# DLRM tower on one Trainium2 core: from pair 8 on, the products with four kept pairs have the batch on partitions and ScalarE sums them

## The reference

```python
e = jnp.stack([tbl_0[ids[:, 0]], ..., tbl_39[ids[:, 39]]], axis=1)   # (512, 40, 64)
i_idx, j_idx = np.triu_indices(40, k=1)
viW = jnp.einsum('bpd,pde->bpe', e[:, i_idx, :], W)                  # W (780, 64, 64)
z = jnp.einsum('bpe,bpe->bp', viW, e[:, j_idx, :])                   # (512, 780)
h = jnp.concatenate([z, dense_ctx], axis=1)                          # (512, 796)
h = jnp.maximum(h @ W_top1 + b_top1, 0.0)                            # (512, 512)
h = jnp.maximum(h @ W_top2 + b_top2, 0.0)                            # (512, 256)
y = h @ W_top3
```

## Time and profile before

| What | Value |
|---|---|
| Median of 3 runs | 370.56 us (369.31 to 371.61) |
| The profiled execution's own time | 369.65 us |
| Its span | 367.8 us |
| TensorE busy (matmul) | 347.9 us, 95% of the span |
| VectorE busy | 259.8 us, 71% |
| ScalarE busy | 38.4 us, 10% |
| GpSimd busy | 154.0 us, 42% |
| Mean granted TensorE clock, share of full speed | 0.991 |

### The profile page before, as it was taken

The page is one execution under the profiler, slowest core; times in us unless marked ns, Lnnn a source line. Parts: engine busy times, 40 slices in busy tenths (PEclk is TensorE's granted clock), DMA queues, the critical chain, the costliest instruction groups (busy, mean ns, idle before and its releaser), DMA issues.

```text
span 367.8 us, 4723 instructions
## 1 busy us (share of the span) xinstructions
PE 347.9 (95%) x1848; PEld 117.8 (32%) x1848; DVE 259.8 (71%) x271; ACT 38.4 (10%) x61; POOL 154.0 (42%) x261
## 2 busy tenths in 40 slices
PE   0999399999999999999999999999999999999997
PEld 0333122333333333333333333333233333333342
DVE  3974971787787877676768877887768787877430
ACT  1011201030100201010010300000000001200132
POOL 6888888027776755344434544243323100000000
PEclk9999879999999999999999999999999999999999
DMA  7378121102641422112112220122022000000000
GB/s 188 139 222 337 22 81 25 27 37 81 223 135 26 130 76 76 16 65 73 46 32 73 70 59 26 65 70 68 12 65 68 5 0 2 0 0 3 0 1 0
DMA packets 11449, 24.29 MB, mean 66 GB/s; under 512 B 3858, under 2 KB 3858, under 8 KB 11299
## 3 DMA queue, kind: packets, MB, share of 16 engines
q1 hardware_dynamic: 7330, 19.79, 16.2%
q0 software_dynamic: 4096, 4.20, 5.4%
HBM read 23.98 MB, written 0.00 MB: 65 GB/s over the span
## 4 chain that ended last, share of the span: by engine, by line
PE 94%; DVE 3%; DMA 1%; issue 1%; ACT 0%; SPq 0%
PE y_ps L472 47%; PE z_ps L495 25%; PE t_ps L424 6%; PE t_ps L451 4%; PE y_ps L503 3%; PE t_ps L442 2%; DVE one_hot L380 2%; PE y_ps L533 2%; PE y_ps L424 2%; PE y_ps L478 2%; DMA ids_all<-in_ids_one_hot 1%; PE t_ps L539 0%; ACT x L315 0%; DVE prod L402 0%; ACT prod L357 0%
## 5 line engine op out<-in xcount | busy, mean ns | idle before, releaser
L402 DVE TENSOR_TENSOR prod<-y_ps,x 128x1024 f32<-128x1024 f32 x190 | 220.9, 1217 | 74.4 <-PE y_ps L472 74.0
L472 PE MATMUL y_ps<-x,w_sb 64*128 64x512 f32 x760 | 180.9, 607 | 0.8 <-issue 0.7
L302 POOL DMA_INDIRECT rows<-in_tbl,ids_sb x128 | 122.6, 958 | 131.4 <-PE y_ps L472 99.1
L472 PEld LDWEIGHTS y_ps<-x,w_sb 64*128 64x128 f32 x760 | 66.7, 186 | 104.3 <-issue 53.3
L495 PE MATMUL z_ps<-prod,selector 128*32 128x512 f32 x780 | 94.9, 602 | 0.0
L495 PEld LDWEIGHTS z_ps<-prod,selector 128*32 128x32 f32 x780 | 20.5, 110 | 67.9 <-issue 34.4
L380 DVE TENSOR_SCALAR one_hot<-ids_all,numbers 128x512 f32<-128x512 int32 x64 | 27.5, 504 | 7.4 <-DMA ids_all<-in_ids_one_hot 7.4
L424 PE MATMUL t_ps<-one_hot,table 128*64 128x512 f32 x96 | 22.9, 633 | 8.8 <-DVE one_hot L380 8.8
L297 POOL MEMSET spacer<- 128x128 f32 x127 | 30.7, 242 | 0.1
L315 ACT ACTIVATE x<-t_ps 128x512 f32<-128x512 f32 x18 | 10.8, 599 | 191.3 <-PE t_ps L442 145.1
L451 PE MATMUL t_ps<-z_sb,w_sb 128*128 128x512 f32 x32 | 15.9, 618 | 0.0
(11 more groups left out here) (30 smaller groups left out, 36.8 us busy)
## 6 DMA issues: line engine op xcount, KB each, us to landing
w_sb<-in_w_units SPq DMA_DIRECT2D x25, 512.0 KB, 3.3
ids_all<-in_ids_one_hot SPq DMA_DIRECT2D x8, 256.0 KB, 4.6
table<-in_small_tables SPq DMA_DIRECT2D x8, 256.0 KB, 5.3
rows<-in_tbl,ids_sb POOLq DMA_INDIRECT x128, 2.5
w_sb<-in_w SPq DMA_DIRECT2D x1, 1792.0 KB, 8.0
w_sb<-in_w SPq DMA_DIRECT2D x1, 512.0 KB, 4.4
ids_sb<-in_ids SPq DMA_DIRECT2D x1, 80.0 KB, 2.2
z_sb<-in_dense_t SPq DMA_DIRECT2D x1, 32.0 KB, 9.5
```

Source lines behind the costliest of these rows:

```text
L302: pool.indirect_dma_start(rows[:, n % ROW_SLOTS, bt, h * D:(h + 1) * D], None, tables[f], bass.IndirectOffsetOnAxis(ap=ids_sb[:, bt, f:f + ...
L402: dve.tensor_tensor(prod[:, at:at + 2, :], y_ps[:, s % Y_SLOTS], leaf, ALU.mult).then_inc(prod_ready, 1)
L472: ins = pe.matmul(y_ps[:, slot, h, :], w_sb[own, c % W_SLOTS, at:at + P], x[own, m, :], start=True, stop=True)
```

## The change

Four pairs, `KEPT` = 1, 3, 5 and 7, keep their gathered rows, with the batch on partitions, in a tile of their own (`kept`). For every k from 8 to 19, the four cross units of k with those pairs are replaced by four "rows" units, one for each block of 128 samples. In a rows unit `x[:, k]` of the block is the weight of the matmul and the matrices (8 partners x 64 columns, tile `w_rows_sb`) are what moves through; the result has the batch on partitions and 8 x 64 columns in each of the slot's two banks. VectorE multiplies it by `kept` into one of 4 slots of `row_prod`. ScalarE then runs 16 copies of 128x64 in place, each with `accum_out` into one column of `z_rows`. Two jobs ("z_turn") of four transposes each bring `z_rows` into two banks of `z_sb`. So 147 units are still summed by the selector (37 rounds), and 48 are rows units; the steps stay 195.

With it go: `w_sb` slots 6 to 4, `rows` slots 6 to 4 beside the kept four, `LEAD` 3 to 5, mix one step earlier, partial jobs every 4 steps, twelve loads of 256 KB for `w_rows_sb` on SyncE's queue, each held until the slot's earlier group is used, and the one-hot tiles share their space with `row_prod`, `w_rows_sb` and `z_rows`. `z_sb` has 7 banks as before.

```diff
+KEPT = (1, 3, 5, 7)
+ROWS_FROM = 8
+ROW_PROD_SLOTS = 4
+ROW_W_SLOTS = 2
-W_SLOTS = 6
+W_SLOTS = 4
-ROW_SLOTS = 6
+ROW_SLOTS = 4
+ROW_LAG = 2
-LEAD = 3
+LEAD = 5
-PARTIAL_EVERY = 6
+PARTIAL_EVERY = 4
 def plan_units():
-        cross = [("cross", m, k) for m in range(k)]
+        own = [("cross", m, k) for m in range(k) if k < ROWS_FROM or m not in KEPT]
         if k % 4 == 3:
-            cross.insert(min(k, 6), ("inner", k // 4))
-        units += cross
+            own.insert(min(k, 6), ("inner", k // 4))
+        if k >= ROWS_FROM:
+            every = (len(own) + BT) // BT if k < NP - 1 else 3
+            for bt in range(BT):
+                own.insert(1 + every * bt, ("rows", k, bt))
+        units += own
...
+    jobs_at[FIRST[ROWS_FROM + GROUPS_IN_BANK] + 8].append(("z_turn", 0))
+    jobs_at[STEPS - 2].append(("z_turn", 1))
...
         def _(act):
+            def sum_rows(s):
+                _, k, bt = UNITS[s]
+                act.wait_ge(prod_ready, s + 1)
+                for h in range(2):
+                    for n in range(2 * len(KEPT)):
+                        own = row_prod[:, NUMBER[s] % ROW_PROD_SLOTS, h, D * n:D * n + D]
+                        column = row_sum(k, h, n)
+                        ins = act.activation(own, own, ACT.Copy, accum_out=z_rows[:, bt, column:column + 1])
+                ins.then_inc(rows_summed, 1)
...
+                if s >= ROW_LAG and UNITS[s - ROW_LAG][0] == "rows":
+                    sum_rows(s - ROW_LAG)
...
         def _(dve):
+                if unit[0] == "rows":
+                    if n >= ROW_PROD_SLOTS:
+                        dve.wait_ge(rows_summed, n - ROW_PROD_SLOTS + 1)
...
+                    leaf = kept[:, unit[2]:unit[2] + 1, :, :].rearrange("p o n d -> p o (n d)").to_broadcast([P, 2, B])
+                    dve.wait_ge(y_ready, s + 1)
+                    dve.tensor_tensor(row_prod[:, n % ROW_PROD_SLOTS], y_ps[:, s % Y_SLOTS], leaf,
+                                      ALU.mult).then_inc(prod_ready, 1)
+                    return
...
         def _(pe):
+                if unit[0] == "rows":
+                    _, k, bt = unit
+                    for h, own in enumerate((low, high)):
+                        ins = pe.matmul(y_ps[:, slot, h, :], x[own, k, P * bt:P * bt + P],
+                                        w_rows_sb[own, (k - ROWS_FROM) % ROW_W_SLOTS, :], start=True, stop=True)
+                    ins.then_inc(y_ready, 1)
+                    return
```

More of the change, by code:

```diff
@@ L74 @@
 STEPS = len(UNITS)
[L75 to L81, removed]
+SUMMED = [s for s, u in enumerate(UNITS) if u[0] != "rows"]
+ROWED = [s for s, u in enumerate(UNITS) if u[0] == "rows"]
+NUMBER = {s: n for units in (SUMMED, ROWED) for n, s in enumerate(units)}
+CHUNKS = -(-len(SUMMED) // CHUNK)
+ROUNDS = -(-len(SUMMED) // ROUND)
+EARLY_BANKS = 2 * PARTIAL_PAIRS
+ROW_BANKS = (EARLY_BANKS, EARLY_BANKS + 1)
+BANKS = EARLY_BANKS + 3
+ROW_GROUPS = NP - ROWS_FROM
+GROUPS_IN_BANK = P // ROW_SUMS
+REST_ROWS = ROW_SUMS * (ROW_GROUPS - GROUPS_IN_BANK)
+DENSE_ROW = REST_ROWS
+assert STEPS == 195 and EARLY_BANKS * BANK_ROUNDS < ROUNDS <= (EARLY_BANKS + 1) * BANK_ROUNDS
+assert len(ROWED) == BT * ROW_GROUPS and REST_ROWS + N_DENSE <= P
 INNER_AT = {u[1]: s for s, u in enumerate(UNITS) if u[0] == "inner"}
@@ L123 @@
 JOBS = [job for at in JOBS_AT for job in at]
-TURNS = [job for job in JOBS if job[0] in ("look", "turn", "partial")]
+TURNS = [job for job in JOBS if job[0] != "mix"]
 TURN_SEQ = {job: n for n, job in enumerate(TURNS)}
@@ L225, in dlrm_tower, with rows_of, rows_ap @@
         out_stored = sem("out_stored")
+        def rows_of(n):
+            if n < len(KEPT):
+                return n, 1
+            return len(KEPT) + (n - len(KEPT)) % ROW_SLOTS, (n - len(KEPT)) // ROW_SLOTS + 1
+        def rows_ap(n, bt):
+            place, _ = rows_of(n)
+            return kept[:, bt, place, :] if n < len(KEPT) else rows[:, place - len(KEPT), bt, :]
         def wait_turn_done(eng, n):
@@ L361, in _ @@
             dve.memset(selector[:], 0.0).then_inc(selector_zeroed, 1)
[L362 removed]
+            dve.memset(z_sb[:, ROW_BANKS[1], :], 0.0).then_inc(z_zeroed, 1)
             dve.wait_ge(selector_zeroed, 1)
@@ L439, in turn @@
                     at = GATHERED.index(job[1])
-                    pe.wait_ge(gathered[at % ROW_SLOTS], 16 * 2 * BT * (at // ROW_SLOTS + 1))
+                    place, use = rows_of(at)
+                    pe.wait_ge(gathered[place], 16 * 2 * BT * use)
                     for bt in range(BT):
-                        ins = pe.transpose(dst[:, P * bt:P * bt + P], rows[:, at % ROW_SLOTS, bt, :], ident[:])
+                        ins = pe.transpose(dst[:, P * bt:P * bt + P], rows_ap(at, bt), ident[:])
+                    ins.then_inc(turned, 1)
+                elif job[0] == "z_turn":
+                    own = slice(P, P + REST_ROWS) if job[1] else slice(0, P)
+                    pe.wait_ge(rows_summed, BT * (ROW_GROUPS if job[1] else GROUPS_IN_BANK))
+                    for bt in range(BT):
+                        ins = pe.transpose(dst[0:own.stop - own.start, P * bt:P * bt + P], z_rows[:, bt, own], ident[:])
                     ins.then_inc(turned, 1)
@@ L549, in lay_out_units @@
     laid = np.zeros((CHUNKS, P, CHUNK, P), w.dtype)
-    for s in range(STEPS):
+    for s in SUMMED:
+        c, at = divmod(NUMBER[s], CHUNK)
         for rows, bank, half, i, j in pairs_of(s):
@@ L553, in lay_out_units, with lay_out_rows @@
             m = w[number[(i, j)]] if i < j else w[number[(j, i)]].T
-            laid[s // CHUNK, D * rows:D * rows + D, s % CHUNK, w_columns(s, bank, half)] = m
+            laid[c, D * rows:D * rows + D, at, w_columns(s, bank, half)] = m
     return laid.reshape(CHUNKS, P, CHUNK * P)
+def lay_out_rows(w):
+    number = pair_numbers()
+    laid = np.zeros((ROW_GROUPS, P, B), w.dtype)
+    for k in range(ROWS_FROM, NP):
+        for h, n, i, j in row_pairs(k):
+            i, j = ORDER[i], ORDER[j]
+            laid[k - ROWS_FROM, D * h:D * h + D, D * n:D * n + D] = (
+                w[number[(i, j)]] if i < j else w[number[(j, i)]].T)
+    return laid
 def lay_out_top1(w):
```

139 lines of the change are left out of this document (95 added, 44 removed).

## The result

The changed kernel takes 377.46 us (376.77 to 378.11, 4 runs) against 370.06 of the kernel before (369.31 to 371.61, 4 runs, one more than in the table above): the ratio is 1.0184, with a 95% interval of 1.0153 to 1.0216, so it is slower by 7.4 us. The forecast was 411 us.

A forecast was written before the change was run, and what follows sets the result against it. TensorE, busy 250.4 of 250.4 us in the changed stretch, bounds the kernel; ScalarE would become the bound. TensorE's -21.1 us and ScalarE's excess of 61.2 us give +40 us, forecast 411 us, range 362 to 470.

The forecast's parts named there:

- The price of a summing copy: On ScalarE in each rows unit: time from one 128x64 accumulating copy to the next, 335 ns, ends 169 and 444 ns.
- the copy itself: ScalarE's 64-column copy without gap or accumulator output: 255 ns, from 628 ns at 512 columns less 373 by the memset's slope.
- The gap of 20 ns: Between ScalarE's copies: 20 ns beyond their own durations, read off four mixes in 2.59 us.
- The accumulator output: On each ScalarE summing copy: the result is written on its own after the last column, taken as 59 ns.
- from one to the next: The spacing of ScalarE's summing copies, built from copy, gap and accumulator output: 335 ns together.
- Rival 1: ScalarE's short copies overlap or are much cheaper than a long one, spacing under 0.233 us: 352 to 366 us; chance 0.22.
- rival 2: ScalarE just fits, spacing 0.233 to 0.257 us: within 1% of now, 367 to 374 us; chance 0.06.
- The per-pair sum: Pairs 8 to 19, each taking the longer of TensorE's and ScalarE's times: ScalarE's excess adds up to 61.2 us.
- TensorE's saving: 48 selector sums of 0.464 us go, two z_turn jobs add 1.16 us: net -21.1 us, largest gain to 346.7 us.
- VectorE still fits, barely: In pair 8, the densest: eight products take VectorE 9.2 us against TensorE's 9.7; more room in each later pair.
- Rival 4: ScalarE harmless, VectorE held by its new waits in pairs 8 to 10: example loss 2.1 us; no chance of its own.
- p: Time from one ScalarE summing copy to the next, likeliest 0.335 us; at 0.24 the per-pair sum gave -1.5 us.

## Why the prediction was wrong

**The price of a summing copy** is the term that was mis-sized, 335 ns forecast, 239 ns measured. The mechanism, ScalarE's queue that takes back what TensorE saves, was right. The parts of the price: the copy itself, 255 ns forecast, 242 measured, was right. The gap of 20 ns was wrong in sign: copies from the same start partition overlap by 96 ns. The accumulator output, 59 ns forecast, adds 93. So 255 + 20 + 59 became 242 - 96 + 93. The error sits in "from one to the next": I read the spacing off rows whose copies change their start partition, and took the least favourable case for all. Rival 1 named the overlap, with its right size, and set its chance by these same rows. Neither side had it whole: the rival had the overlap without the readout, the forecast the readout without the overlap. The measured 239 ns lies in the narrow band of rival 2 (chance 0.06), whose 367 to 374 us were 3.5 us too low.

**The per-pair sum** does well once it is given 239 ns. It then has an excess of ScalarE of 19.2 us; the runs with all sums and with one differ by 23.0. The 4 us between are not taken apart. The place of a copy inside a pair, which a sum per pair can't see, is the likeliest: moving the sums by five steps was worth 7.5 us. The half clock and the unnamed 2 us before the save may lie in them too. The forecast put the copies behind about one rows unit's sums, with its lead of five steps; the copy of pair 10 stands behind the sums of all of pair 8 and one of pair 9, 5 x 3.8 us.

**TensorE's saving** was 21.1 us forecast and 16.0 measured with one sum. The prices of a sum, a turn and a partial job held; the error sits in the units' pace, 4.8 us more for the 161 units of the stretch (154.3 against 149.5). What failed is "VectorE still fits, barely": I set VectorE's eight products (9.2 us) against TensorE's time per pair, and left out that VectorE idles 1.2 us at each sum however many products stand between the sums. Rival 4 said that this decides nothing by itself; it took 2.9 us.

**Put together:** -21.1 + 5.1 (VectorE's pace and an open rest) + 23.0 (ScalarE) = +7.0, and +7.4 was measured. The last two are differences of runs, so the sum has to come out; it shows the sizes of the errors and proves nothing more. With the right p but the forecast's own sum it would have been -2: the two smaller errors decided the sign, the large one the distance. That the kernel is slower at all, as forecast, is partly luck.

**The signs named for the trace after:** gaps on TensorE in pairs 8 to 13 and none in 17 to 19, right. 588 summing records, right. Rows units at 0.86 to 0.96 us where nothing holds them, right. ScalarE over 70% busy, 59%, and copies 0.3 us apart, 0.24. VectorE's idle time before row products released by ScalarE: 1.5 us once, wrong; the hold is TensorE's wait for `x`. "A second instruction per copy, of any length above 0.1 us, puts it above 430": it is 188 ns long and adds 93, so a duration was taken for a spacing.

**The range,** 362 to 470, held the time; the forecast of a clear move to 411 was more than five times too large. Two readings of rows were slightly off and mattered little. Four products in 4.62 us start (4.62 - 1.22) / 3 = 1.13 us apart, not 1.155. And four mixes in 2.59 us leave (2.59 - 4 x 0.628) / 3 = 26 ns between two, not 20.

## What to carry to other kernels

Work moved to an idle engine is paid at that engine's densest stretch: count it against the time between two of its old jobs that others wait for, not against its idle share, and place it behind those jobs on the queue. Here the same idea lost 7.4 us from pair 8 with sums at once, and won 13.4 us from pair 10 with sums put off and the turns moved ahead; how much each of these three did wasn't separated, and pair 8 with both wasn't run. Read the spacing of short instructions from neighbours with the same start partition, and price an accumulator output by what it adds to the spacing (here 93 ns), not by its duration (188 ns).

## What the runs showed of the hardware

- ScalarE: copies of 128x64 are 242 ns long and 146 ns apart from one start partition; 64x64 copies from alternating start partitions are 255 ns long and 266 ns apart. An increment on each makes no difference.
- ScalarE: an accumulator output is an instruction of 188 ns of its own, which adds 93 ns to the spacing.
- TensorE: in and after a hold of 6.3 us the granted clock was 0.50 to 0.52 (120 to 128 us); after the hold of 2.0 us with half of the sums, the windows there had 0.79; with three repeats after a hold of 1.9 us it was 0.57 (120 to 124 us). What the half clock costs the changed kernel by itself is some 2 us, 0 to 4 by the intervals.
